# Layer 2's filter: the last six of 22 blocks of each tile squared by GpSimd instead of VectorE

## The reference

```
sim   = tanh(adj * adj)
filt  = sim * (adj > 0)                    # = tanh(max(adj, 0) * adj)
keep the 700 largest of each row           # no row here has that many
h2    = tanh(h @ W_proj + b_proj)
feat  = relu(new_adj @ (h2 @ W_gcn) + b_gcn)
x     = x + feat
```

## Time and profile before

| | |
|---|---|
| median of 3 runs | 2302.53 us (2302.17 to 2304.77) |
| profiled execution, span from first to last instruction | 2300.6 us |
| PE busy | 1991.3 us (87%) |
| DVE busy | 1567.9 us (68%) |
| ACT busy | 1097.9 us (48%) |
| POOL busy | 449.8 us (20%) |

### The profile page before, as it was taken

One profiled execution on the slowest core, in us unless ns is written; L12 is line 12 of the kernel. 1 busy time (PEld: TensorE's weight loads), 2 busy tenths in 40 slices (PEclk: granted clock), 3 DMA queues, 4 the chain that ended last, 5 costly groups with the idle time before them and its releaser, 6 DMA issues.

```text
span 2300.6 us, 42794 instructions
## 1 busy us (share of the span) xinstructions
PE 1991.3 (87%) x16187; PEld 1354.2 (59%) x16187; DVE 1567.9 (68%) x3124; ACT 1097.9 (48%) x2149; POOL 449.8 (20%) x455
## 2 busy tenths in 40 slices
PE   6999286999999999939995799759967999999788
PEld 3887263678888888827763588647754222222333
DVE  6766665654455468765668799545567999999565
ACT  7454275522222235417764678336555224242655
POOL 0000474100000013217761100157620000000000
PEclk9999697999999999969997899879988999999899
DMA  7999367556565679765756477333232432322000
GB/s 206 328 354 322 122 154 162 210 211 235 216 227 223 237 265 403 290 220 168 235 181 176 101 194 196 134 122 94 84 111 70 122 117 86 90 83 91 1 17 33
DMA packets 236975, 396.26 MB, mean 172 GB/s; under 512 B 20640, under 2 KB 189217, under 8 KB 220514
## 3 DMA queue, kind: packets, MB, share of 16 engines
q1 hardware_dynamic: 211974, 340.97, 44.7%
q0 software_dynamic: 15296, 43.88, 7.2%
q10 hardware_dynamic: 9504, 8.65, 1.2%
HBM read 309.88 MB, written 83.56 MB: 171 GB/s over the span
## 4 chain that ended last, share of the span: by engine, by line
PE 58%; DVE 22%; DMA 8%; ACT 5%; issue 4%; POOL 2%; SPq 1%; ACTq 0%; DVEq 0%; POOLq 0%
PE ps L1037 9%; PE ps L1039 9%; PE ps L1038 9%; DVE BIG L2683 7%; PE ps L273 4%; PE ps L274 4%; PE ps L275 4%; PE ps L2184 4%; PE ps L2505 4%; DMA BIG<-in_adjT 3%; PE ps L2186 2%; PE ps L2511 2%; DMA X<-rows_split,idxg 2%; PE ps L2160 1%; DVE BIG L2678 1%
## 5 line engine op out<-in xcount | busy, mean ns | idle before, releaser
L1037 PE MATMUL ps<-R,BIG 128*128 128x256 f16 (+1 forms) x1936 | 530.8, 274 | 10.3 <-DVE BIG L1609 5.9
L1039 PE MATMUL ps<-R,BIG 128*128 128x256 f16 (+1 forms) x1936 | 527.9, 273 | 0.0
L1038 PE MATMUL ps<-R,BIG 128*128 128x256 f16 x1936 | 527.7, 273 | 0.0
L2505 PE MATMUL ps<-BIG 128*64 128x452 f32 x1056 | 230.8, 558 | 24.1 <-DVE BIG L2683 20.4
L1037 PEld LDWEIGHTS ps<-R,BIG 128*128 128x128 f16 x1936 | 187.6, 97 | 43.8 <-issue 13.2
L1038 PEld LDWEIGHTS ps<-R,BIG 128*128 128x128 f16 x1936 | 189.8, 98 | 22.9
L1039 PEld LDWEIGHTS ps<-R,BIG 128*128 128x128 f16 x1936 | 188.0, 97 | 26.0
L2683 DVE SCALAR_TENSOR_TENSOR BIG<-BIG 128x904 f32<-128x904 f32 x176 | 192.4, 1155 | 1.6
L2567 ACT ACTIVATE BIG<-X,BIG 128x64 f32<-128x64 f32 x264 | 70.2, 337 | 233.0 <-PE ps L2511 233.0
L2505 PEld LDWEIGHTS ps<-BIG 128*64 128x64 f32 x1056 | 64.3, 136 | 186.7 <-issue 131.2
L2184 PE MATMUL ps<-BIG,X 128*128 x464 | 157.2, 385 | 9.6 <-DVE X L2243 9.6
(11 more groups left out here) (393 smaller groups left out, 4494.1 us busy)
## 6 DMA issues: line engine op xcount, KB each, us to landing
BIG<-adj_split SPq DMA_DIRECT2D x66, 1408.0 KB, 6.3
BIG<-in_adjT SPq DMA_DIRECT2D x42, 1408.0 KB, 11.7
adj_split<-BIG SPq DMA_DIRECT2D x22, 1408.0 KB, 9.8
BIG<-in_adj SPq DMA_DIRECT2D x22, 1408.0 KB, 10.3
BIG<-in_adjT SPq DMA_DIRECT2D x66, 452.0 KB, 3.3
XX<-in_f SPq DMA_DIRECT2D x70, 256.0 KB, 7.7
experts_split<-XX SPq DMA_DIRECT2D x64, 256.0 KB, 4.4
BIG<-experts_split SPq DMA_DIRECT2D x16, 1024.0 KB, 12.9
```

Source lines behind the costliest of these rows:

```text
L1037: pe.matmul(out[:, 0:n], pr[:, 0, k, :], h[:, k, 0:n], start=start, stop=False)
L1038: pe.matmul(out[:, 0:D], pr[:, 0, k, :], l[:, k, 0:D], start=False, stop=False)
L1039: return pe.matmul(out[:, 0:n], pr[:, 1, k, :], h[:, k, 0:n], start=False, stop=stop)
L2505: pe.matmul(ps[rs, 2 * (h // 2) + c, 0:CW], self.G[:, u, h * HF:(h + 1) * HF], self.PT[:, u, h, cs], start=start, stop=stop)
```

## The change

GpSimd squares blocks 16 to 21 of each tile (6 x 128 = 768 elements), VectorE blocks 0 to 15 (2048 elements). GpSimd does it with two instructions, the maximum with zero (one input) and the product with itself (two inputs), with a wait on its own semaphore between them. ScalarE's tanh waits for both parts, by the semaphores `r` and `rq`. GpSimd works on tiles 0 to 3 ahead of its loop, and in round t on tile t + 3, after the root.

```diff
             def pool(self, pool):
                 s = self.st
-
+                for t in range(4):
+                    self.square_rest(pool, t)
                 for t in range(KT + 1):
                     if t >= 1:
                         s.wait(pool, "ag", t)
                         root_pool(pool, (t - 1) % 4, 1, s)
+                    if t and t + 3 < KT:
+                        self.square_rest(pool, t + 3)
                     if t == KT - 5:
                         zero_tail(pool, s)

             def tanh(self, act, t):
                 a = aslot(4 + t % 3)
                 self.st.wait(act, "r", t + 1)
+                self.st.wait(act, "rq", t + 1)
                 act.activation(a, a, ACT.Tanh).then_inc(self.st["nn"], 1)
...
+            BY_DVE = 16
+
+            def raw_ready(self, eng, t):
+                self.st.wait(eng, f"d{4 + t % 3}", 16 * (t // 3) + 16)
+                if t == KT - 1:
+                    self.st.wait(eng, "zp", 1)
+
             def square(self, v, t):
-                s, a = self.st, aslot(4 + t % 3)
-                s.wait(v, f"d{4 + t % 3}", 16 * (t // 3) + 16)
-                if t == KT - 1:
-                    s.wait(v, "zp", 1)
-                v.scalar_tensor_tensor(a, a, 0.0, a, ALU.max, ALU.mult).then_inc(s["r"], 1)
+                a = aslot(4 + t % 3)[:, 0:self.BY_DVE]
+                self.raw_ready(v, t)
+                v.scalar_tensor_tensor(a, a, 0.0, a, ALU.max, ALU.mult).then_inc(self.st["r"], 1)
+
+            def square_rest(self, pool, t):
+                a = aslot(4 + t % 3)[:, self.BY_DVE:KT]
+                self.raw_ready(pool, t)
+                pool.wait_ge(po.sem, po.inc(pool.tensor_scalar(a, a, 0.0, None, ALU.max)))
+                pool.tensor_tensor(a, a, a, ALU.mult).then_inc(self.st["rq"], 1)
```

More of the change, by code:

```diff
@@ L1514, in __init__ @@
                 self.rows = Rows(E1, 4 * D, ["bg", "bias"])
-                self.st = Stage("seq", **{f"d{4 + u}": 16 * len(range(u, KT, 3)) for u in range(3)}, r=KT, nn=KT, zp=1,
+                self.st = Stage("seq", **{f"d{4 + u}": 16 * len(range(u, KT, 3)) for u in range(3)}, r=KT, rq=KT, nn=KT, zp=1,
                                 hi=KT, lo=KT, used=KT, ev=KT, ag=KT, le=KT, t=KT, **Rows.totals())
```

## The result

Five runs of the changed kernel: median 2432.86 us (2430.84 to 2437.47), against 2302.53 of the kernel before in the same runs; the ratio is 1.0556, 95% interval 1.0539 to 1.0572. Slower, as forecast, but by 130 us and not by 33, and far outside the range. The profiled span is 2430.9 against 2300.6, 130.3 more. Of all the runs of this document one is left out, the second of experiment e2, which took 3510.70 us at a granted clock of 0.553.

The account below looks back on a forecast made before the run. PE was taken as the bound by a hair, 8.03 us per tile. Rounds of 20.3 us per two against 15.9, and round 17, gave 39.1 us more; less 6.0 at the end, plus 0.4: 2336 us, range 2316 to 2352.

Parts of the forecast that it names:

- First, the two engines shut each other out: VectorE's two-input instructions and GpSimd's SBUF reads: whichever is issued first holds the other out for the whole instruction.
- Who gets in at a change: Between VectorE's split and square, the waiting GpSimd instruction gets in first.
- A short round: Round whose split input is ready: GpSimd's pair and VectorE hold each other out; next round opens at 9.8 us.
- a long round: Following round: split waits for the late copy until 4.95 us, GpSimd's pair runs unhindered; next round at 10.5 us.
- For the maximum the trace has no row of that size: GpSimd's maximum of 768 elements taken as 0.91 us, between bounds of 0.67 and 1.64.
- PE has its slack back to give: From round 18's opening to the last sum, 24.6 us instead of 30.59: 6.0 us less.
- Nearly all of it lies under PE's 8.03 us: The 0.8 us saved on each of VectorE's 22 squares, 17.6 us, mostly buys nothing because PE sets the pace.
- Ahead of round 1: First squares' savings and first pairs' hold-ups put at 0, between -2 and +3 us; stage before, a rounded 0.4.
- B: Rival, not slower: engines alternate finely, VectorE's round averages 7.7 us, PE stays the bound; 2301 to 2303 us, 9%.
- C: Rival, faster: B, and the stage's fill gets 0.8 to 5 us shorter; 2297 us, 3%.
- D: Rival, partial: engines hold each other out only while inputs are read, 0.8 to 1.3 us per round; 2312 to 2324, 8%.
- E: Rival, worse: maximum as slow as the product or slower, and PE's clock falls in its gaps; 2347 to 2362 us, 6%.

Follow-up runs that it names:

- e2: Changed kernel, but GpSimd's pair for tile t + 3 stands ahead of the wait for round t's statistics, not behind the root: 2322.08 us, 1.0082.
- e10: Changed kernel, but VectorE squares all 22 blocks and GpSimd's pair, same place and wait, works on one scratch column: 2409.64 us, 1.0453.
- e5: Changed kernel, but VectorE squares all; GpSimd's pair works on 768 scratch elements in rounds 1 to 18, and no engine waits for it: 2337.47 us, 1.0132.
- e11: e2 with a second product in place of GpSimd's maximum: 2337.06 us, 1.0131.
- e1: Changed kernel, but ScalarE's normalising of tile t - 2 stands ahead of tanh and copy of tile t + 3: 2350.62 us, 1.0192.
- e8: Kernel before the change, with ScalarE's normalising ahead of tanh and copy as in e1: 2306.55 us, 1.0002.
- e4: Changed kernel without GpSimd's maximum; the product squares without the positive part: 2388.14 us, 1.0389.
- e6: Changed kernel without GpSimd's pair: VectorE squares blocks 0 to 15, blocks 16 to 21 stay unsquared: 2304.21 us, 0.9985.
- e7: Changed kernel, but GpSimd squares the last 2 blocks of 22 instead of 6: 2419.06 us, 1.0495.

## Why the prediction was wrong

**"First, the two engines shut each other out": right in kind, in one direction too strong.** VectorE holds GpSimd for its whole instruction, whatever GpSimd's size (2.75 and 2.89 us for one element, e10). GpSimd holds VectorE for a time that goes with what it reads and not with its length (e5, e11). A sign of it stood in the earlier trace rows: when L1095 began, POOL's first instruction had 0.79 us to run, so a hold to its end would have made L1095 1.21 us long, and it took 1.00. Who gets in at a change was right: the waiting maximum enters between split and square, 1340.4.

**"A short round" and "a long round": the step that failed, and most of the miss.** I followed the pair to tanh, copy and the split, which is one round later, and stopped there. The instructions queued behind ScalarE's copy in its own list, L1085 and L1091, I left out, though the diff puts a wait ahead of them. They belong to a tile five earlier and release L1095 of the *same* round. So the loop closes in one round: product's end at sum + 8.88, tanh and copy 5.1, normalising 1.03, L1095 and the next sum 0.4, 15.4 in all, where I had 20.3 for two. e1 takes that one order away, and the short and the long round appear; e8 shows that the order had been harmless. Between the changed kernel and e1 stand 82 of the 97 us by which I missed. That the pair of rounds in e1 also has my length is the luck told above.

**"For the maximum the trace has no row of that size": mis-sized.** 2.12 to 2.14 us alone against my 0.91 and my bounds of 0.67 and 1.64; the product was 1.47 against 1.64. In the closed chain the maximum counts in full and more: 2.8 us per round (e4), its own 2.14 and some 0.6 for which the product, which now comes after the square has begun, waits for the square's end. The Trainium skill ("GPSIMD Engine Reference", section "Engine selection") calls one-input operations roughly line rate, an estimate of 0.64 us here from its 1.2 GHz. The runs disagree, with more than three times as much.

**"PE has its slack back to give": wrong.** I put the end at 6.0 us less; it was 8.1 more, 14.1 of the 97 us, and still 2.8 more in e1. The last pair is held out in round 18 like the others (4.67 us in e1, at 1490.60), and tile 21's split is late for its copy.

**"Nearly all of it lies under PE's 8.03 us": right.** The square is 0.80 shorter and e6 buys 0.15%.

**Ahead of round 1: put at 0 and a rounded 0.4, measured 2.8, and not shown to be the change's.** The roots of the stage before, which stand ahead of every changed instruction, already come 4.2 later in this profile (1262.05 against 1257.83). And e8, where nothing ahead of round 1 costs more than before, opens round 1 at 1316.01, 4.8 later than the profile before, with a time that is the same (1.0002). So profiles differ here by more than the 2.8. What moves them I did not find out.

**The rivals.** B and C fell with e2, where the chain is open and 0.8% remains. D was right about the mechanism, in the direction from GpSimd to VectorE: it put a round at 0.8 to 1.3 us more and the time at 2312 to 2324, and e2, the kernel in which nothing else acts, has 1.1 us more and 2322. I had given it 8%. E had the right condition, a maximum slower than the product, but not the price. It also named PE's clock in its gaps: it is granted at 0.83 between 1340 and 1360 us in the kernel after and at 1.00 in e2. PE isn't in the chain of 15.49 us, so that cost nothing in the rounds. None of the rivals was a closed loop.

What the 130 us consist of, by the runs: the place of the pair with one element 104 (e10), and moving the 768 elements into it some 24. With the place put right, some 19 are left (e2, 1.0082). The parts don't add up to a sum, since in the chain an instruction costs its length and out of it only its reading.

## What to carry to other kernels

When work moves to an idle engine, ask of every engine that now waits what else is queued behind the wait in its list, of whatever tile, and follow that until the loop closes, and then look for the next loop. What sets the round is the loop with the most time per round that it spans (here 15.4 us over one round, against the 20.3 over two that I had found), not the first found. Put the new work ahead of any wait it doesn't need: here one call moved up is worth some 109 of the 130 us (1.0556 against e2's 1.0082). And before the move, time the kernel with the work simply left out: e6 would have said that there was 0.15% to win.

## What the runs showed of the hardware

**GpSimd holds VectorE for its reading alone, 0.82 ns per input element.** VectorE's instruction with two inputs in SBUF grows beside GpSimd's by 0.63 us for a maximum of 768 elements (2.28 to 2.91, e2), by 0.19 to 0.21 for one of 256 (e7, a square of 2560: 2.81 to 2.83 alone, 3.02 beside it), and by 1.26 to 1.28 for a product with 2 x 768 inputs (L1095 in e2, the squares in e4, e5 and e11). Divided by the inputs, the larger two are 0.82 or 0.83 ns, and the small one is that within its reading. It is a hold and not a fine alternation: L1095 has 256 elements of its own and still gave way for all 1536 of the product's reads. That it is the reading that holds is inferred from this count; no row shows the reads themselves.

Writing doesn't hold: GpSimd's memset of the earlier trace rows, 2.01 us from 1440.56, ran inside a split that took its usual 3.08 (VectorE's timeline before):

```profile
1440.18 3.08 DVE L1609 TENSOR_TENSOR BIG<-BIG 128x2816 f16<-128x2816 f32 x1
```

The Trainium skill ("SBUF — State Buffer", section "Who interferes with whom") calls the shared ports an exclusive lock, and exempts a GpSimd instruction that only writes. With the exemption the trace agrees. A lock for the whole instruction, as I had read it, the runs show in one direction only: held for the whole maximum, the square of e2 would have taken 2.1 us more and not 0.63, and e11 would have been faster than e2, where it is slower (1.0131 against 1.0082, rounds 9.72 against 9.07).

**GpSimd's maximum with zero is slower than its product.** 2.14 against 1.47 us for 768 elements of float32 (timeline after, 1325.03 and 1327.25), one input against two. I know of no reason for it from these runs.

**Beside a VectorE that runs two-input instructions back to back, a small GpSimd instruction lasts until the one that VectorE runs has ended**, and the next one, if it waits for the first, can miss the change and be out for another: 5.7 us for two elements (e10).
